# Folding plane sums on TensorE and moving planes from VectorE to ScalarE in the statistics stage of a gated norm and column scan

## The reference

```python
mean = jnp.mean(xf, axis=-1); mx = jnp.max(xf, axis=-1); std = jnp.std(xf, axis=-1, ddof=1)
u = jnp.stack([mean, mx, std], axis=-1)
med = jnp.median(u.reshape(b, -1), axis=-1)[:, None, None]
z = jnp.einsum('bck,ck->bc', (u - med) ** 3, cfc_w)
z = z / jnp.sqrt(1.0 + BN_EPS) * bn_w + bn_b
return x * jax.nn.sigmoid(z)[:, :, None, None]      # x = x + this, three times, each on _gn(x)
```

## Time and profile before

| | |
|---|---|
| median of three runs | 910.0 us (908.2, 910.0, 911.15) |
| profiled execution: device time | 909.22 us |
| profiled execution: span from the first to the last instruction | 907.5 us |
| VectorE's copy of the means into `stat` (L616) starts at | 57.42 us |
| busy share of the span: PE, DVE, ACT | 86%, 76%, 48% |

### The profile page before, as it was taken

How to read it: one execution, slowest core, us unless ns; L and a number is a source line. 1 busy time by engine, 2 the same in 40 slices (tenths; PEclk the granted TensorE clock), 3 DMA queues, 4 the chain that set the end, 5 groups by cost and what they waited for, 6 DMA issues and landing times.

```text
span 907.5 us, 12847 instructions
## 1 busy us (share of the span) xinstructions
PE 780.0 (86%) x3604; PEld 629.9 (69%) x3604; DVE 688.7 (76%) x1410; ACT 433.8 (48%) x1380; POOL 36.3 (4%) x68
## 2 busy tenths in 40 slices
PE   0022336999999999999999999999999999999996
PEld 0021224888888888888888888888888888888885
DVE  7977668666766776667766777888888887888887
ACT  6974441444444444444444444444444444444444
POOL 2003420000000000000000000000000000000002
PEclk9996556999999999999999999999999999999998
DMA  8930020000000000000000013332223333332223
GB/s 350 420 159 0 0 94 23 1 1 0 0 0 0 0 0 0 0 0 0 0 0 0 0 46 92 92 92 81 70 80 92 92 92 92 92 92 74 72 85 116
DMA packets 71513, 56.79 MB, mean 63 GB/s; under 512 B 1872, under 2 KB 67408, under 8 KB 69456
## 3 DMA queue, kind: packets, MB, share of 16 engines
q1 hardware_dynamic: 71072, 56.63, 18.8%
q10 hardware_dynamic: 432, 0.07, 0.0%
HBM read 39.91 MB, written 16.78 MB: 62 GB/s over the span
## 4 chain that ended last, share of the span: by engine, by line
PE 85%; DVE 12%; issue 1%; ACT 1%; DMA 1%; ACTq 0%; DVEq 0%
PE ps_prods L530 25%; PE ps_prods L534 25%; PE ps_prods L533 25%; PE ps_turns L542 6%; DVE half_max L610 4%; DVE below_flags L662 2%; PE ps_values L501 2%; DVE bn_parts L605 2%; DMA x_sb<-x_cols 1%; DVE under L668 0%; DVE x_sb L760 0%; PE ps_second L483 0%; PE ps_group L480 0%; DVE t L593 0%; DVE rstd L594 0%
## 5 line engine op out<-in xcount | busy, mean ns | idle before, releaser
L530 PE MATMUL ps_prods<-w_hi,s_hi 128*128 128x512 f32 x992 | 402.2, 405 | 0.3 <-DVE s_lo L750 0.3
L533 PE MATMUL ps_prods<-w_lo,s_hi 128*128 128x512 f32 x992 | 401.4, 405 | 0.0
L534 PE MATMUL ps_prods<-w_hi,s_lo 128*128 128x512 f32 x992 | 391.2, 394 | 0.0
L456 ACT ACTIVATE act_buf<-ps_prods 128x256 f32<-128x256 f32 x248 | 81.9, 382 | 358.8 <-PE ps_prods L534 355.8
L760 DVE SCALAR_TENSOR_TENSOR x_sb<-act_buf,x_sb 128x256 f32 (+1 forms) x248 | 107.3, 433 | 156.3 <-ACT act_buf L462 145.7
L530 PEld LDWEIGHTS ps_prods<-w_hi,s_hi 128*128 128x128 f32 x992 | 186.9, 188 | 39.1 <-DVE s_lo L750 1.1
L534 PEld LDWEIGHTS ps_prods<-w_hi,s_lo 128*128 128x128 f32 x992 | 187.2, 189 | 38.4
L533 PEld LDWEIGHTS ps_prods<-w_lo,s_hi 128*128 128x128 f32 x992 | 187.6, 189 | 32.8
L462 ACT ACTIVATE act_buf<-ps_turns,bias 128x128 f32<-128x128 f32 x496 | 157.6, 377 | 50.8 <-PE ps_turns L542 50.8
L468 ACT ACTIVATE ps_below<-ps_turns,neg_bias 128x128 f32<-128x128 f32 x496 | 153.0, 363 | 0.0
L767 DVE SCALAR_TENSOR_TENSOR x_sb<-ps_below,neg_slope,x_sb 128x256 f32 (+1 forms) x248 | 119.3, 481 | 4.9
(11 more groups left out here) (116 smaller groups left out, 321.3 us busy)
## 6 DMA issues: line engine op xcount, KB each, us to landing
x_sb<-x_cols SPq DMA_DIRECT2D x16, 1024.0 KB, 21.3
stage<-x_cols SPq DMA_DIRECT2D x31, 512.0 KB, 4.1
out_cols<-x_sb SPq DMA_DIRECT2D x31, 512.0 KB, 4.8
w_raw<-w_t SPq DMA_DIRECT2D x8, 512.0 KB, 21.5
x_sb<-x_cols SPq DMA_DIRECT2D x1, 2048.0 KB, 7.9
x_sb<-x_cols SPq DMA_DIRECT2D x1, 512.0 KB, 4.0
out_cols<-x_sb SPq DMA_DIRECT2D x2, 256.0 KB, 2.3
params<-gates ACTq DMA_DIRECT2D x1, 60.0 KB, 5.3
```

The source lines that it names most:

```text
L456: act.activation(act_buf[:, half], ps_prod[c][:, half], ACT.Copy).then_inc(raw_copied, 1)
L530: pe.matmul(ps_prod[c], s_hi[:, k, :], w_hi[:, k, w_cols], start=(k == 0), stop=False)
L533: pe.matmul(ps_prod[c], s_hi[:, k, :], w_lo[:, k, w_cols], start=False, stop=False)
L534: return pe.matmul(ps_prod[c], s_lo[:, k, :], w_hi[:, k, w_cols], start=False, stop=(k == CT - 1))
```

## The change

TensorE gets work in the statistics stage. For channel tiles 1 to 6 (`SUMMED`) it adds up the 32 columns of ScalarE's planes eight to one: eight matmuls with the identity as the stationary operand (one for each group of 4 columns, a *quad*) accumulate in one half of the PSUM tile `ps_below`, which is then 4 columns wide for each image. ScalarE's Copy pass then reads 128 values in PSUM instead of 1024 in SBUF. Ten bf16 matmuls (`keep_warm`) run ahead of these. The Square passes are as before. Tiles 0 and 7 keep the long Copy pass.

`vector_images` becomes 1, 1, 0, 1, 1, 0, 1, 2 for tiles 0 to 7, which is 7 planes for VectorE and 25 for ScalarE: six planes go to ScalarE (one each of tiles 0, 4 and 6, one of tile 5, two of tile 2) and one of tile 7 comes back.

```diff
         def vector_images(ct):
 
-            return 2 - ct % 2
+            return 2 if ct == CT - 1 else 0 if ct in (2, 5) else 1
+
+        SUMMED = range(1, CT - 1)
+        ps_sums = [ps_below[:, r * 512:(r + 1) * 512] for r in range(2)]
+
+        def sums_by_image(ct):
+
+            images = N - vector_images(ct)
+            return ps_sums[ct % 2][:, 0:4 * images * H].rearrange("p (w n h) -> p n w h", w=4, n=images)
...
@@ ScalarE
-            def plane_sum(n, ct, func, out, **affine):
+            def plane_sum(plane, func, out, **affine):
...
-                act.activation(waste[passes % 2], x_sb[:, ct, :, n * H:(n + 1) * H], func,
+                act.activation(waste[passes % 2][:, 0:plane.shape[1], :], plane, func,
...
+                if ct in SUMMED:
+                    act.wait_ge(quads_summed, ct - SUMMED[0] + 1)
                 for n in mine:
-                    plane_sum(n, ct, ACT.Copy, mean_var[:, n, ct, 0:1], scale=1.0 / PIX)
+                    plane = sums_by_image(ct)[:, n - mine[0], :, :] if ct in SUMMED else plane_of(n, ct)
+                    plane_sum(plane, ACT.Copy, mean_var[:, n, ct, 0:1], scale=1.0 / PIX)
...
@@ TensorE
+            def keep_warm(count, bank):
+
+                for _ in range(count):
+                    pe.matmul(bank[:, :], ones_bf[:, :], ones_bf[:, :].unsqueeze(1).broadcast_to([P, 4, P]),
+                              start=True, stop=True)
+
+            pe.wait_ge(x_loaded[0][0], 16)
+            keep_warm(10, ps_group)
+            for ct in SUMMED:
+                if ct - SUMMED[0] >= 2:
+                    pe.wait_ge(act_shift_done, ct - 1)
+                first = vector_images(ct) * H
+                for b in range(2):
+                    pe.wait_ge(x_loaded[ct][b], 16)
+                    for quad in range(4 * b, 4 * b + 4):
+                        last = pe.matmul(ps_sums[ct % 2][:, 0:4 * (NH - first)], ident[:, :],
+                                         x_sb[:, ct, 4 * quad:4 * quad + 4, first:NH],
+                                         start=(quad == 0), stop=(quad == 7))
+                last.then_inc(quads_summed, 1)
```

More of the change, by code:

```diff
@@ L158, in gated_norm_and_column_scan_kernel @@
         act_shift_done = sem("act_shift_done")
+        quads_summed = sem("quads_summed")
         params_loaded = sem("params_loaded")
@@ L396, in plane_sum, with plane_of @@
                     act.wait_ge(act_summed, passes - 1)
-                act.activation(waste[passes % 2], x_sb[:, ct, :, n * H:(n + 1) * H], func,
+                act.activation(waste[passes % 2][:, 0:plane.shape[1], :], plane, func,
                                accum_out=out, **affine).then_inc(act_summed, 1)
                 passes += 1
+            def plane_of(n, ct):
+                return x_sb[:, ct, :, n * H:(n + 1) * H]
             for ct in range(CT):
@@ L412, in _ @@
                 for n in mine:
-                    plane_sum(n, ct, ACT.Square, mean_var[:, n, ct, 1:2], scale=PIX ** -0.5,
+                    plane_sum(plane_of(n, ct), ACT.Square, mean_var[:, n, ct, 1:2], scale=PIX ** -0.5,
                               bias=mean_div[:, n, ct:ct + 1])
@@ L605, in _ @@
                         last = dve.bn_stats(bn_parts[:, ct, n, b, :], x_sb[:, ct, cols, n * H:(n + 1) * H])
-                    if b == 1:
+                    if b == 1 and vector_images(ct):
                         link(last)
```

## The result

The changed kernel takes 912.03 us (median of 22 runs, 910.06 to 914.23) against 910.03 us for the kernel before in as many runs: a ratio of 1.0019, 95% interval 1.0013 to 1.0025. By this ratio it is 1.7 us slower (1.2 to 2.3); the two medians lie 2.0 us apart. That is more than nothing and less than the 0.3% that the prediction took as its bound. The forecast was +0.5 us, 910.5 within 905.6 to 914.5. The result lies in that range, on the slower side, and just outside the forecast's own 908.2 to 912.

What follows compares the result with a forecast made beforehand. The copy of the means, waiting for both VectorE and ScalarE, was taken as the bound: 57.7 us against 57.42, +0.3 us. On the 910.0 us median that gives 910.3, set at 910.5 for dearer short passes; range 905.6 to 914.5.

Steps and rivals of the forecast that it cites:

- the forecast: Statistics stage: sums cost 0.60 to 0.68 us, clock up within 3 us of the first; -1.8 to +2 us, chance 0.42.
- What bounds the kernel: Before the scan: VectorE and ScalarE are nearly equal bounds; less work on VectorE alone gains at most 0.8 us.
- VectorE: Statistics stage: losing six planes and getting one, VectorE ends at 51.4 us, 6 us earlier.
- ScalarE's passes: Statistics stage: a short Copy pass costs 0.30 us against 1.04; 42.6 us of work against 46.5.
- TensorE's price: Sums before the scan: 0.65 us for an fp32 matmul of 384 columns, so TensorE is slower than the loads.
- The lower bound: Sums before the scan: an fp32 matmul of 384 columns costs at least 0.35 us, from the scan's matmul spacing.
- The clock: Start of tile 1's sums: ten bf16 matmuls of 4.3 us raise the clock to 2.4 GHz despite 2.2 us idle.
- rival B: Statistics stage: clock rises 3.4 to 6.8 us after the first sum; +2.0 to +3.7, up to +5 us; chance 0.20.
- A: Statistics stage: a sum matmul costs 0.35 us, ScalarE waits only for tiles 1 and 2; -4.3 us; chance 0.26.

Runs made afterwards that it cites:

- e4: Changed kernel with the old split of planes (VectorE 2 and 1 in turn), only the sums kept: 908.66 us, ratio 0.9999 to the kernel before.
- e5: Changed kernel with long Copy passes in all tiles, sums made but not waited for: 917.23 us, ratio 1.0093 to the kernel before.
- e7: The changed kernel again, unaltered, beside other runs on one chip: 910.98 us, ratio 1.0024 to the kernel before.
- e1: Changed kernel with 16 bf16 matmuls ahead of the sums in place of 10: 908.68 us, ratio 1.0004 to the kernel before.
- e2: Changed kernel without the ten bf16 matmuls ahead of the sums: 911.51 us, ratio 1.0032 to the kernel before.
- e3: Changed kernel with the sums in bf16, from the upper halves of the fp32 words: 904.61 us, ratio 0.9960 to the kernel before.
- e6: Changed kernel with sums for tiles 2 to 6 only, 9 planes on VectorE, 38 bf16 matmuls ahead: 905.37 us, ratio 0.9968 to the kernel before.
- e8: Changed kernel with sums for tiles 2 to 6, 38 bf16 matmuls, 8 planes on VectorE (none of tile 1): 904.49 us, ratio 0.9955 to before.

## Why the prediction came out as it did

**What bounds the kernel: right.** Both engines had to be relieved together: e4 relieves ScalarE alone and gains nothing, e5 moves planes alone and costs 8.5 us. And the time follows the copy of the means, as the prediction took it. Against the kernel before, in us:

| | copy starts (profiled execution) | time (by the ratio) |
|---|---|---|
| changed kernel, e7 | +1.9, +1.7 | +1.7, +2.2 |
| e1, e2 | +0.3, +2.8 | +0.4, +2.9 |
| e3 | -4.7 | -3.6 |
| e4, e5 | +0.2, +9.1 | -0.1, +8.5 |
| e6, e8 | -3.0, -3.8 | -2.9, -4.1 |

**VectorE: right.** 51.4 us were worked out, 51.5 measured.

**ScalarE's passes: right.** 0.30 us for a short pass, 0.28 measured, from the difference of two like passes; the nearest row that read PSUM (377 ns) would have been too dear. The 8.6 us that were expected of e5 (8.5 measured) came from the same addition.

**TensorE's price: right.** 0.65 us was worked out for 384 columns in fp32, from the spacing of two transposes. In the changed kernel at 2.4 GHz the sums' weight loads lie 0.43 us apart for records of 512 columns:

```profile
21.58 0.19 PEld L509 LDWEIGHTS ps_below<-x_sb,ident 128*128 128x128 f32 x1 [0.24 <-issue]
22.01 0.19 PEld L509 LDWEIGHTS ps_below<-x_sb,ident 128*128 128x128 f32 x1 [0.24 <-issue]
22.44 0.19 PEld L509 LDWEIGHTS ps_below<-x_sb,ident 128*128 128x128 f32 x1 [0.24 <-issue]
```

That is 0.86 us for a matmul with 512 columns (0.87 predicted), or 1024 columns a record at 2.4 GHz, twice what it has. Four passes for fp32, as the Trainium skill has it (FP8 and Floating Point Precision, TensorE Precision Notes): now the trace agrees, with these 0.43 us. The lower bound, 0.35 us from the matmuls of the scan, wasn't the pattern to follow: their weights are fp32r, and 512 columns take 0.23 us in one record, where fp32 takes two records of 0.43.

**The clock: wrong, and it is nearly the whole loss.** The prediction said: "So the clock should be up, just, when tile 1 lands. It is the narrowest step of this working." In the profiled execution of the changed kernel it had risen early, at 9.1 us, and fell again at 12.5, just as the sums began. The row that should have warned was the prediction's own, a fall 2.6 us after the transposes' end, against a gap of 2.2 us; the early rise shortened the ten matmuls to 3.79 us (4.42 in e7) and made the gap 2.58. The first sums ran at half speed for 3.4 us, which delays TensorE by 1.7 us. 0.3 + 1.7 is 2.0, and 1.9 were measured at L651. e1 closes the gap and finds +0.3 us at L651 and almost no difference in time; e2 widens the loss.

That is rival B by its mechanism, at the lower end of its prices, and close to the edge of the forecast, which allowed 3 us of low clock. B's 3.4 to 6.8 us from the first sum to the rise came from no row; measured were 3.0 (e7), 3.4 (the changed kernel), 5.4 (e2) and 6.0 us (e5). Its dearer end is +5 in the text on B and +4.5 in the range, which doesn't touch the outcome.

**The same ten matmuls don't give the same clock.** Five profiled executions have them ahead of the sums. In e4 the clock was up at the first sums, as predicted. In the changed kernel and in e3 it fell as they began, and in e5 and e7 it hadn't risen yet. So the step fails in part of the executions and not in all, and the time of one execution is in part luck.

**A chance was badly placed.** B had 0.20, against 0.68 for A and the forecast together, though both profiled executions of the changed kernel show a low clock at the first sums. A step called the narrowest one, on which 1.7 us hang, should have moved the predicted time by a part of them.

## What to carry to other kernels

Before work goes to an idle engine, lay its rate beside the rate at which the data land: TensorE needed 2.6 to 3.4 us for a half tile that lands each 2.5 us, so each tile given to it made it later. One tile less, no tile with all four planes among the summed ones, and bf16 matmuls up to the first sum (e8) together turned 1.7 us of loss into 4.1 us of gain. Where two engines end together, a change must take from both, and it is judged by the later of the two ends, not by the work removed. And warm-up matmuls must reach the work that they are for: cover the gap to the first real matmul, or expect to pay for the low clock in a part of the executions.

## What the runs showed of the hardware

- The fp32 sums without pauses had 1.00 from 15.9 us to their end. The bf16 sums, with 0.5 to 1.6 us of idleness before each half tile, had a granted clock of 0.53 over 12 us. A faster matmul can so leave TensorE at its lower clock.
- Ten bf16 matmuls, the same in five kernels, left the clock at the first sums up once (e4) and low four times; where they reached to within 0.9 us of the first sum (e1, e6, e8), it was up in all three profiled executions.
- The scan, the same code in all kernels, took 754.7 to 754.9 us in the profiles of before, e3, e6 and e8, and 755.8 to 756.6 in the other six. The granted clock is 1.00 in it in both the kernel before and the changed one, and the loss is spread evenly: from 200 to 800 us, windows of 200 us hold 932, 934 and 932 matmul records in the kernel before and 930 each in the changed one. In e1, e2, e4, e5 and e7 the profiled execution is the slowest of its kernel, in e3 and e6 the fastest, which suggests that the long scan goes with the execution and not with the kernel. It doesn't show it: e8's profiled execution is its slowest too and has a short scan. What makes the 0.2% isn't known; a difference between two profiled spans has to be taken apart by stage before it is put down to the change.
